# A chain of four attention layers in a software pipeline: rows replicated by DMA, an epsilon tile in place of a constant, and a listed place for every step of every group

## The reference, cut to what matters

```python
def attention(x, keys, Wq, bq, Wk, bk, Wv, bv):
    q, k, v = x @ Wq + bq, keys @ Wk + bk, keys @ Wv + bv
    return softmax(q @ k.T / 16) @ v

x = attention(x, ctx, L0) @ Wo + bo + x                        # L0
t = x + sum(attention(ln(x), ln(keys), L1a or L1v) @ Wo + bo   # L1, keys = ctx and side
            for the two)
x = ln(t) @ fc_W + fc_b + t
x = ln(x + softmax(q @ k.T / 16, over the queries) @ v)        # L2 (eps 1e-6)
x = x + attention(x, ctx, L3) @ Wo + bo                        # L3
```

## Time and profile before

| | us |
|---|---|
| median of 3 runs | 613.43 |
| the profiled execution | 613.34 |
| its span, first to last instruction | 611.5 |
| TensorE busy, 4872 matmuls | 582.3 (95%) |
| VectorE busy | 537.5 (88%) |
| ScalarE busy | 431.5 (71%) |
| GpSimd busy | 520.0 (85%) |
| mean granted clock of TensorE | 0.993 |

### The profile page before, as it was taken

The page is one execution under the profiler, slowest core; times in us unless marked ns, Lnnn a source line. Parts: engine busy times, 40 slices in busy tenths (PEclk is TensorE's granted clock), DMA queues, the critical chain, the costliest instruction groups (busy, mean ns, idle before and its releaser), DMA issues. The chain is left out here.

```text
span 611.5 us, 16892 instructions
## 1 busy us (share of the span) xinstructions
PE 582.3 (95%) x4872; PEld 567.7 (93%) x4872; DVE 537.5 (88%) x1685; ACT 431.5 (71%) x1473; POOL 520.0 (85%) x694
## 2 busy tenths in 40 slices
PE   4889999899999999999999999999999999999985
PEld 4778999899999999999999999999999899999974
DVE  1457789999999999999999999999999999989993
ACT  2546967777777778778777777877876788677443
POOL 3268887898999999999999999999999999867763
PEclk9998999999999999999999999999999999999999
DMA  8512211003222211122222221112333020000012
GB/s 274 217 62 70 82 48 46 3 1 96 80 78 80 78 56 51 54 80 79 78 80 79 79 79 53 48 60 78 114 104 114 17 89 28 18 3 19 19 35 70
DMA packets 28076, 42.80 MB, mean 70 GB/s; under 512 B 2513, under 2 KB 19793, under 8 KB 27985
## 3 DMA queue, kind: packets, MB, share of 16 engines
q1 hardware_dynamic: 27986, 41.72, 20.6%
HBM read 33.32 MB, written 8.39 MB: 68 GB/s over the span
## 5 line engine op out<-in xcount | busy, mean ns | idle before, releaser
L720 ACT ACTIVATE prob_L<-bank,neg_max_L 128x128 f32<-128x128 f32 x320 | 114.1, 379 | 70.1 <-DVE neg_max_L L952 69.7
L1082 POOL TENSOR_SCALAR xhat_ln<-x,rstd_ln,shift_ln 128x256 f32<-128x256 f32 x128 | 71.1, 564 | 14.0 <-issue 7.4
L652 ACT ACTIVATE oT_hi_L<-bank 128x256 fp32r<-128x256 f32 (+1 forms) x128 | 55.9, 460 | 34.4 <-PE bank L476 34.4
L720 ACT ACTIVATION_READ_ACCUMULATOR prob_L<-bank,neg_max_L 128x1 f32 x320 | 69.1, 216 | 0.0
L952 DVE TENSOR_REDUCE neg_max_L<-bank 128x2 f32<-128x256 f32 (+1 forms) x128 | 59.0, 477 | 11.5 <-PE bank L470 11.1
L652 ACT ACTIVATE xT_hi_L<-bank 128x512 fp32r<-128x512 f32 (+1 forms) x96 | 59.5, 620 | 7.4 <-PE bank L448 7.1
L854 DVE TENSOR_TENSOR oT_lo_L<-bank,oT_hi_L 128x256 fp32r<-128x256 f32 (+1 forms) x128 | 58.7, 478 | 2.9 <-ACT oT_hi_L L652 2.8
L1076 POOL TENSOR_TENSOR rstd_ln<-var_eps_ln,minus_half 128x2 f32<-128x2 f32 x64 | 45.3, 708 | 12.6 <-DVE var_eps_ln L919 7.4
L1116 POOL TENSOR_TENSOR xT_lo_L<-x_in,xT_hi_L 128x512 fp32r<-128x512 f32 x32 | 41.0, 1282 | 12.2 <-ACT xT_hi_L L652 12.2
L652 ACT ACTIVATE probT_L<-bank 128x256 f32<-128x256 f32 (+1 forms) x96 | 47.4, 495 | 4.3 <-PE bank L454 4.1
L985 DVE TENSOR_TENSOR x<-bank,x_bias 128x512 f32<-128x512 f32 x64 | 43.8, 685 | 6.5 <-PE bank L489 4.3
(11 more groups left out here) (217 smaller groups left out, 2390.9 us busy)
## 6 DMA issues: line engine op xcount, KB each, us to landing
x_in<-in_x SPq DMA_DIRECT2D x32, 512.0 KB, 4.2
ctx_in<-in_ctx SPq DMA_DIRECT2D x32, 256.0 KB, 4.3
out<-y SPq DMA_DIRECT2D x32, 256.0 KB, 2.2
side_in<-in_side SPq DMA_DIRECT2D x32, 128.0 KB, 2.5
WqT_L<-in_L_WqT SPq DMA_DIRECT2D x3, 256.0 KB, 4.3
Wo_L<-in_L_Wo SPq DMA_DIRECT2D x2, 256.0 KB, 4.7
WkT_L<-in_L_WkT SPq DMA_DIRECT2D x3, 128.0 KB, 4.1
WvT_L<-in_L_WvT SPq DMA_DIRECT2D x2, 128.0 KB, 4.0
```

The costliest lines, as they stand in the source:

```text
L652: activation(to, of, ACT.Copy).then_inc(done[step], 1)
L720: last = activation(at(prob[k], g)[:, b, :], block(bank, b), ACT.Exp, bias=at(neg_max[k], g)[:, b:b + 1], accum_out=at(total[k], g)[:, b:b ...
L1082: last = pool.tensor_scalar(at(to, g)[:, n, :], tile, at(rstd[k], g)[:, n:n + 1], at(shift[k], g)[:, n:n + 1], ALU.mult, ALU.add)
```

## The change

Four things change.

**Rows by DMA.** Each vector that was spread by a matmul is now loaded 128 times by one DMA into a [128, width] tile. The bias of a layer is the PSUM product plus that tile, one addition on VectorE. `L2_bv` and `L3_g1` (gamma) are loaded straight to where they are used, and the gains of the L1 keys are multiplied into WkT on GpSimd. The loads wait on semaphores of their own (`qk`, `vo`, cols, rows). SyncE now issues, in this order: L0's WqT and WkT, cols, L0's WvT and Wo, one row, x of group 0, then 25 loads of weights and rows, then ctx of group 0 as the 33rd, and up to ctx of group 9 before x of group 3.

**Epsilon tile.** Line 919 adds a [128, 4] tile filled with epsilon, by tensor_tensor, in place of a constant by tensor_scalar.

**No shift.** The `shift` tiles and the three steps `shift_keys`, `shift_ln1`, `shift_ln2` go. `normalised` computes (x - mean) * rstd with the same number of instructions.

**Places.** `STARTS` has a list of 32 times for each step, `COMES` is gone, and each single product, copy and load of the preparation has its own time. The times of the middle groups are 1687.6 units apart; in the first four and in the last ten groups every step has another distance to its neighbours.

```diff
-STARTS = {"load_x": 0, "hi_L0": 107, "lo_L0": 281, "load_ctx": 580, "Q_L0": 626, "hi_ctx": 640, "q_L0": 727,
...
-COMES = [0, 810, 1589, 3179, 4746, 6323, 7901, 9478, 11056, 12634, 14212, 15790, 17368, 18945, 20523, 22101, 23679,
...
-PREPARATIONS = {"load_first": -50, "constants": -40, "keys_L0": 81, "products_L0": 284, "vectors_L0": 406,
...
+    "Q_L0": [897, 2530, 3041, 3669, 5111, 5747, 8357, 9020, 11913, 13672, 15360, 17047, 18735, 20422, 22110, 23798, 25485,
+        27173, 28860, 30548, 32236, 33794, 35535, 37126, 38999, 39636, 42380, 43222, 44184, 46198, 47152, 48204],
...
+    "S_L0": [2112, 2674, 3185, 3952, 5456, 6992, 8861, 10636, 12346, 14106, 15793, 17481, 19168, 20856, 22544, 24231, 25919,
+        27606, 29294, 30982, 32669, 34281, 35916, 37612, 39389, 41197, 42884, 43588, 44640, 46675, 47606, 48844],
...
+    "OUT_L3": [11245, 12391, 13048, 14780, 16424, 18111, 19799, 21486, 23174, 24862, 26549, 28237, 29924, 31612, 33266, 34886,
+        36688, 38128, 40095, 42451, 43632, 45575, 47651, 49865, 51935, 53690, 55148, 55813, 56142, 56676, 57093, 57630],
...
+    "store": [11595, 12622, 13361, 15098, 16622, 18309, 19997, 21684, 23372, 25060, 26747, 28435, 30122, 31810, 33606, 35137,
+        37116, 38315, 40580, 42641, 43954, 46054, 47940, 50133, 52194, 53974, 55439, 56153, 56379, 56863, 57280, 57817],
...
+PREPARATIONS = {"M_L0": 395, "N_L0": 528, "m_L0": 484, "n_L0": 615, "M_L1a": 969, "N_L1a": 1058, "m_L1a": 1145, "M_L1v": 1234, "N_L1v":
...
+    "load_qk_L0": 70, "load_cols": 82, "load_vo_L0": 88, "load_rows_L0": 100, "load_qk_L1a": 112, "load_gains": 124,
...
-    table = [(STARTS[name] + COMES[g], g, name) for name in STARTS for g in range(GROUPS)]
-    table += [(PREPARATIONS[name], -1, name) for name in PREPARATIONS]
+    table = [(times[g], g, name) for name, times in STARTS.items() for g in range(GROUPS)]
+    table += [(time, -1, name) for name, time in PREPARATIONS.items()]
...
+            def replicated(to, r, what):
+                n, width = ROWS.index(r), to.shape[1]
+                sp.dma_start(to[:], ins["rows"][n:n + 1, 0:width].to_broadcast([P, width])).then_inc(weights[what], 16)
...
-                terms += [(ones_row[:], row(r)) for r in extra]
...
+            def bias_plus(key, to, use, added):
+                dve.tensor_tensor(to[:], bank_of(use)[:, 0:D], added[:], ALU.add).then_inc(done[key], 1)
...
-                dve.tensor_scalar(at(var_eps[k], g)[:], mv[:, :, 1], eps, None, ALU.add).then_inc(done[f"var_{k}"], 1)
+                if g == 0:
+                    prepared(dve, "constants")
+                dve.tensor_tensor(at(var_eps[k], g)[:], mv[:, :, 1], epsilon[eps][:, 0:len(tiles)], ALU.add).then_inc(done[f"var_{k}"], 1)
...
-            def shift_of(k):
-                def of(g):
-                    dve.wait_ge(done[f"rstd_{k}"], g + 1)
-                    earlier(dve, f"norm_{k}", g, len(shift[k]))
-                    dve.scalar_tensor_tensor(out=at(shift[k], g)[:], in0=at(mean_var[k], g)[:, :, 0], scalar=-1.0,
-                                             in1=at(rstd[k], g)[:], op0=ALU.mult, op1=ALU.mult).then_inc(done[f"shift_{k}"], 1)
-                return of
...
-                    last = pool.tensor_scalar(at(to, g)[:, n, :], tile, at(rstd[k], g)[:, n:n + 1], at(shift[k], g)[:, n:n + 1],
-                                              ALU.mult, ALU.add)
+                    last = pool.tensor_scalar(at(to, g)[:, n, :], tile, at(mean_var[k], g)[:, n, 0:1], at(rstd[k], g)[:, n:n + 1],
+                                              ALU.subtract, ALU.mult)
```

More of the change, by code:

```diff
@@ L88 @@
-SMALL = [f"{what}_{k}" for what in ("stats", "mean", "var") for k in ("keys", "ln1", "lnf", "ln2")] + ["x_gamma"]
-SIGNALS = {"TensorE": {"keys_L1": ["gain_L1a", "gain_L1v"], "products_L0": ["M_L0", "N_L0"], "vectors_L0": ["m_L0", "n_L0"],
[13 rows of a table removed]
+EMPTIED_BY |= {"m_L0": "m_col_L0", "n_L0": "bias_L0", "m_L1a": "m_col_L1a", "m_L1v": "m_col_L1v", "n_L1": "bias_L1", "n_fc": "bias_fc",
+               "mean_fc": "centred_fc", "M_L2": "M_lo_L2", "k_L2": "k_bias2", "m_L3": "m_col_L3", "n_L3": "bias_L3"}
+EMPTIED_BY |= {f"{w}_{a}": f"{w}_lo_{a}" for w in "MN" for a in ATTENTIONS}
@@ L106, in timetable @@
+SMALL = [f"{what}_{k}" for what in ("stats", "mean", "var") for k in ("keys", "ln1", "lnf", "ln2")] + ["x_gamma", "zeroed"]
 def timetable():
-    table = [(STARTS[name] + COMES[g], g, name) for name in STARTS for g in range(GROUPS)]
-    table += [(PREPARATIONS[name], -1, name) for name in PREPARATIONS]
+    table = [(times[g], g, name) for name, times in STARTS.items() for g in range(GROUPS)]
+    table += [(time, -1, name) for name, time in PREPARATIONS.items()]
     return sorted(table)
@@ L188, in build @@
             layer_buffers(k)
-        stats, mean_var, var_eps, rstd, shift = ({} for _ in range(5))
+        stats, mean_var, var_eps, rstd = ({} for _ in range(4))
         for k, n in {"keys": A["L1"] * GROUP, "ln1": GROUP, "lnf": GROUP, "ln2": GROUP}.items():
@@ L313, in load_rest, with two @@
-            def load_rest():
-                weights_of("L1a")
-                weights_of("L1v")
-                weights_of("L2")
-                sp.dma_start(Wv2[:], ins["L2_Wv"]).then_inc(weights["L2"], 16)
-                sp.dma_start(fcW[:], ins["fc_W"].rearrange("(t p) n -> p t n", p=P)).then_inc(weights["fc"], 16)
-                weights_of("L3")
+            def two(a, first, second, what):
+                for w in (first, second):
+                    sp.dma_start(stage[a][w][:], ins[f"{a}_{w}"].rearrange("(t p) n -> p t n", p=P)).then_inc(weights[f"{a}_{what}"], 16)
@@ L372, in products @@
                     last.then_inc(done[f"N_{a}"], 1)
+                return of
             def query_bias(a):
-                bank = bank_for(pe, f"m_{a}")
-                terms = [(stage[a]["WkT"][:, h, :], col(f"{a}_bq", h, scaled_cols)) for h in range(T)]
-                if a in LN:
-                    prepared(pe, f"M0_{a}")
-                    terms += [(M0[a][:, e, :], col(f"{a}_b1", e, scaled_cols)) for e in range(T)]
-                for n, (stationary, moving) in enumerate(terms):
-                    last = mm(bank[:, 0:1], stationary, moving, start=n == 0, stop=n == len(terms) - 1)
@@ L413, in fc, with of @@
-            def fc():
-                pe.wait_ge(weights["fc"], FC_WEIGHTS)
+                def of():
+                    prepared(pe, "scaled")
+                    pe.wait_ge(weights[f"{a}_qk"], TWO)
+                    if a in LN_KEYS:
+                        prepared(pe, f"gained_{a}")
+                    bank = bank_for(pe, f"m_{a}")
+                    terms = [(stage[a]["WkT"][:, h, :], col(f"{a}_bq", h, scaled_cols)) for h in range(T)]
+                    if a in LN:
+                        prepared(pe, f"M0_{a}")
+                        terms += [(M0[a][:, t, :], col(f"{a}_b1", t, scaled_cols)) for t in range(T)]
+                    for n, (stationary, moving) in enumerate(terms):
+                        last = mm(bank[:, 0:1], stationary, moving, start=n == 0, stop=n == len(terms) - 1)
+                    last.then_inc(done[f"m_{a}"], 1)
@@ new lines, in query_bias, with output_bias, of @@
+                return of
+            def output_bias(key, attentions):
+                def of():
+                    bank = bank_for(pe, f"n_{key}")
+                    terms = []
+                    for a in attentions:
+                        prepared(pe, f"rep_{a}")
+                        pe.wait_ge(weights[f"{a}_vo"], TWO)
+                        terms += [(rep[a]["bv"][:, h, :], stage[a]["Wo"][:, h, :]) for h in range(T)]
+                        if a in LN_KEYS:
+                            prepared(pe, f"N0_{a}")
+                            terms += [(rep[a]["b2"][:], N0[a][:])]
+                    for n, (stationary, moving) in enumerate(terms):
+                        last = mm(bank[:, 0:D], stationary, moving, start=n == 0, stop=n == len(terms) - 1)
+                    last.then_inc(done[f"n_{key}"], 1)
+                return of
@@ L415, in fc, with n_fc @@
+            def n_fc():
+                pe.wait_ge(weights["fc"], ONE)
                 prepared(pe, "rep_fc")
                 bank = bank_for(pe, "n_fc")
-                terms = [(rep["fc"]["bv"][:, t, :], fcW[:, t, :]) for t in range(T)] + [(ones_row[:], row("fc_bias"))]
-                for n, (stationary, moving) in enumerate(terms):
-                    last = mm(bank[:, 0:D], stationary, moving, start=n == 0, stop=n == len(terms) - 1)
+                for t in range(T):
+                    last = mm(bank[:, 0:D], rep["fc"]["bv"][:, t, :], fcW[:, t, :], start=t == 0, stop=t == T - 1)
```

384 lines of the change are left out of this document (212 added, 172 removed), and 200 rows, old and new, of tables (COPIES, PREPARATIONS, SIGNALS, STARTS).

## The result

The changed kernel takes 715.58 us (median of 4 runs, 714.74 to 717.2), the kernel before 613.66 in the same comparison: ratio 1.1665, interval 1.1639 to 1.1692. Forecast were 597 us and faster. It is 102 us slower.

The account below looks back on a forecast made before the run. TensorE was taken to set the pace, at 17.00 us a group, with GpSimd and VectorE nearly full. Terms -5.3 - 2.0 + 0.8 - 2.6 - 5.0 - 1.8 = -15.9 gave 597 us; range 587 to 609.

Parts of the forecast that it names:

- the part on the epsilon tile and the shift: Small VectorE steps: epsilon's addition 1.6 us and the shift 0.7 us a group lighter; 0 gained between 200 and 400 us.
- The slower rival: GpSimd becomes the bound because late operands hold up its fixed order; period 17.6 us, time 616 us, chance 0.12.
- The listed order: A place of its own for every step of every group: fewer float32r entries and fewer TensorE waits; -2.6, -5.0 and -1.8 us.
- -2.6 for fewer entries: TensorE's steady period: seven entries into float32r blocks a group instead of eight, 0.08 us each over 32 groups.
- -5.0 for waits: TensorE from 100 to 580 us: most of its 5.8 us of idle goes, as the table leaves gaps of 1.5 us.
- the -1.8 that follows from them: TensorE from 100 us on: with fewer waits fewer matmuls run singly, so 1.8 us of busy time goes.
- the sign that I had named: TensorE's idle time between 100 and 580 us: below 1.5 us confirms the new order, above 6 refutes it.
- The rule that I weighed: Trainium skill: a VectorE operation with two SBUF inputs is held for a running GpSimd operation; epsilon's 1.6 us would stay.
- the 400 that I had named as proof: Epsilon's addition on VectorE taking above 400 ns would prove the skill's rule on holds by GpSimd.
- The -1.6 us a group: Epsilon's additions on VectorE fall to 155 ns each with the tile, saving 1.6 us of VectorE's work a group.
- the start in sum: Preparation: one-row matmuls gone -5.3 us, first product's weights issued first -2.0, first context loaded later +0.8.
- The issue time: SyncE's queue: each load issue takes 0.53 us by the trace, where the new table gives 0.06.

Follow-up runs that it names:

- e2: The kernel before with only the normalization changed to (x - mean) * rstd on GpSimd, without the shift, in its old order of steps; 711.21 us against 615.07.
- e1: The changed kernel with the shift put back on VectorE and x * rstd + shift on GpSimd, its new list of places kept; 662.35 us, ratio 1.077.
- e3: The kernel before with rows by DMA and the epsilon tile, the shift kept, in the old order of steps; 621.49 us, ratio 1.0117.
- e11: The changed kernel with the shift restored, new list's places up to 30 us, old places from 80 us, a glide between; 608.99 us against 614.28, ratio 0.9914.
- e15: e11 with the steps of all four compute engines in groups 10 to 25 in the new list's order within the period; 653.7 us, ratio 1.0641.

## Why the prediction was wrong

**The step that failed** is in the part on the epsilon tile and the shift: "GpSimd's normalization now takes mean and rstd with the same count of operations". I counted instructions and priced the new pair of operations by the old pair's row, at no change. It went from 564 to 1230 ns, together 4.1 us a group on an engine with 0.9 us to spare. In the old order this alone costs 96 us (e2) and gives the period of the changed kernel. The trace of before shows no `tensor_scalar` on GpSimd that subtracts, so the price should have been bounded from both sides: 564 ns below, and above the tensor-tensor operations there:

```profile
L1132 POOL TENSOR_TENSOR x_bias<-x,bias_L 128x512 f32<-128x512 f32 x32 | 41.2, 1287 | 0.0
```

That they come near the truth is luck, as they have twice the elements; but four operations a group at that price are 2.9 us more, and would have shown a GpSimd that does not fit into 17.0 us.

**The slower rival** named the right engine with the wrong mechanism: GpSimd became the bound by work and not by waits. Its price, 616 us, is a loss of 3 us where there were 102. The sum is also a little low by its own terms: from the forecast period of 16.92 to 17.6 it is 0.68 us and not 0.6 a group, and 619 us.

**The listed order** was the second failed step: -2.6 for fewer entries and -5.0 for waits, with the -1.8 that follows from them. TensorE's order by itself gave 610.7 against 609.0, with seven entries and a period of 17.00 us: the entries go and the time stays. With the shift in place the list costs 662.35 - 608.99 = 53 us instead, and by the sign that I had named (above 6 us of idle TensorE from 100 to 580 us) e1 refutes it with 36 us. I read the table's gaps on TensorE (1.5 us) as a promise, though I had found its load issues priced at 0.06 for 0.53 us and knew VectorE's held additions at 730 ns from the earlier trace rows. The list has no room for a hold. It gives x3's bias 0.78 us to VectorE's next step, and in e1's timeline it takes 1.64; it gives lnf's statistics with epsilon's addition 1.21 us, and the addition alone takes 1.25. I counted on 14.5 us of VectorE work a group; it is 15.7 in the changed kernel and 17.7 in e1, the shift included.

**The rule that I weighed** against the trace was right where it bore on the change. I took x3's bias, median 480 against 468, as "mostly not held", with GpSimd busy 94%. It was mostly not held because the old order sets it beside the power; the row said something of its place, not of the operation. Epsilon's addition went to 557, 517 and 319 ns in the mean, above the 400 that I had named as proof on two of three. The -1.6 us a group for it stayed away: e3 has 746, 480 and 290 ns in the old order.

**Right** were the start in sum (one-row matmuls, first weights, later context, together -6.5; e11 gained 5.3, with the first matmul 3.5 us earlier where 2.0 were counted), ctx's issue at 17.6 (17.75), the count of 4852, and that rows and epsilon cost nothing in the steady part. The issue time, 0.53 us, was rightly the price of a place in a long row of loads; for one load alone it is small, as a context takes 4.3 us to land.

**The sum as measured** depends on the order in which the parts are taken. Start first: -5; the listed order with the shift +53; the shift's removal with its slow pair +53; together 101. With a fast pair the removal gives 22 back, and the pair costs 75. Pair first: +96 in the old order, and all the rest together 4. So the pair is enough to explain the result, and the listed order's loss shows in full only when the pair is gone.

**Open.** How the 53 us of the listed order divide between VectorE's holds (VectorE's work grew by 1.4 us a group, the period by 2.1) and the waits in the chain to rstd was not separated: moving epsilon to ScalarE took 22 of them, and put a longer chain in. The list's places for the last ten groups were not tried by themselves. A listed order with only the power moved beside x3's bias was not tried.

## What to carry to other kernels

Price an operation by its own row, kind by kind: on GpSimd the same `tensor_scalar` is 554 ns or 1220, by whether it subtracts, so write `x + (-m)` or fold the mean into a shift (here the first was faster in the listed order, 640.73 against 662.35, and slower in the old one, 621.3 against 613.8). A list of places is as good as its durations: one that gives every VectorE operation a fixed time is off where GpSimd works beside it, so take what runs next to what from a trace, and put held kinds beside the power or a multiply-add, if the engine that runs those has time to spare. Where a change rearranges everything, take its start and its steady part separately; here the start alone, joined to the old steady order, beat both kernels.

## What the runs showed of the hardware

- GpSimd `tensor_scalar` on 128x256: 554 ns for two of add and multiply, 0.92 us for one alone, 1.07 to 1.22 us for a pair with a subtraction; on 128x128 450 against 797 ns. From 128 to 256 columns that is 0.8 ns a column more for the fast pair (450 to 554) and, by the means of the changed kernel, 3.4 for the slow one (797 to 1230).
- A VectorE constant addition, tensor-tensor or scalar-tensor-tensor operation on SBUF that comes up while GpSimd adds 128x512 waits for its end: in e1's timeline above an addition of two numbers ends 0.01 us after it; beside such additions 8 small ones took 2.84 to 3.88 us instead of 0.68. Statistics' aggregation (0.64 for 8) and reciprocal (0.59) are not held, and GpSimd's power holds none of them.
- GpSimd is held in turn: six of its 128x512 additions took 7.35 us, and 7.88 beside VectorE's 128x256 operations with two SBUF inputs. The power that makes rstd of lnf has a median of 987 ns in the kernel before, where x3's bias is already running when it begins, and 715 in e15, where it is not.
